# Loads, column halves and unit order of the first stage rewritten in a fused attention and feed-forward kernel

## The chip, the cores and the metric

The kernel runs on one Trainium2 chip, on all 8 cores at once; each core takes one batch element of 2048 tokens and runs the same program, with no exchange between cores. The metric is the device time in microseconds (us) of the slowest core. Lower is better.

## The reference

Per batch element, with 2048 tokens, width 1024, 16 heads of 64 and a hidden width of 3072:

```python
xn = _layernorm(x, axis=-1)
x = x + _L0_attn_ref(xn, W_attn, b_attn, W_proj, b_proj, temperature) + _L0_ffn_ref(xn, w_gate, w_up, w_down)
...
# attention: causal, with ALiBi slopes
qkv = x @ W_attn + b_attn
att = jnp.einsum('bqhd,bkhd->bhqk', q, k) * scale / temperature + bias
y = jnp.einsum('bhqk,bkhd->bqhd', softmax(att), v)
return y @ W_proj + b_proj
# feed-forward: weights are int8-valued integers times 1/127
h = _silu(x @ wg.T) * (x @ wu.T)
return h @ wd.T
```

## The kernel before, in words

The program has three stages. The **first stage** makes everything that attention starts from. The **second stage** (a long list of steps written by a planner, `attention_plan`) interleaves attention of 16 heads with 88 of the 96 gate-and-up units of the feed-forward part. The **third stage** is the output: the projection and the down product. The change touches the first stage and, on GpSimd, what the second one begins with.

In the first stage the 2048 tokens are 16 tiles of 128. For tile i the steps are these, each on another engine, tied by semaphores:

- SyncE loads the fp32 tile into one of four buffers `xstage` (semaphores `l_x0` to `l_x3`). Tile i, from 4 on, may be loaded once tile i-4 has been normalised (`v_xn`).
- VectorE takes the statistics (two `bn_stats`, one `bn_aggr`), ScalarE the square root into `sd`, VectorE the reciprocal into `rs`, and then it writes the normalised bf16 tile `xn_st`. Below this last one is called the normalisation of tile i.
- TensorE transposes the tile by eight matmuls with the identity into `ps_s` (even tiles) or `ps_gu` (odd ones): "transpose i", signalled by `p_xT`. ScalarE evacuates it into `xnT` (`a_xe`).
- TensorE multiplies 128 tokens of `xnT` by half of the value weights (512 columns of `wv_b`): a "V unit" of eight matmuls of 512 columns into `ps_t`. There are 32 of them, two halves for each of 16 tiles. ScalarE evacuates each into `Vt`.
- For every block of 512 tokens TensorE makes q and k of the first pair of heads from `wqk_b`: 16 matmuls, eight into `ps_m` and eight into `ps_y`, called QK 0 to QK 3. VectorE evacuates q (`evac_q`, `qst`), ScalarE k (`evac_k`, `kst`), and SyncE copies both to `qx` and `kx`.

All weights come by DMAs issued from GpSimd (POOL), which cast fp32 to bf16: the two halves of `wv_b` (128 x 4096 each), `wqk_b` for two pairs of heads, the first two sets of gate and up weights (`wgbuf`, `wubuf`), and `wpj_b` for the projection. GpSimd also sets constant rows of `qx` and `kx` by 12 memsets. The DMAs of SyncE and GpSimd are served by the same 16 DMA engines, from two queues.

Each engine runs its instructions in the order in which they are written, so the order of the code is the order of the work. Before the change, TensorE's loop does in pass i transpose i, then the V units of tile i-1; for tiles 0 to 3 only the first half, and their second halves together in pass 4, behind QK 0. ScalarE's loop does in pass i the square root of tile i, then the evacuation of transpose i-2. VectorE does in pass i the statistics of tile i, then the normalisation of tile i-1; `evac_q` stands behind the normalisations of tiles 5, 9 and 13 and at the end.

Of the kernel before, what the change touches and what calls it, by code (L numbers as in the profile page):

```python
# [11 lines left out]
I32 = mybir.dt.int32  # L12
AF = mybir.ActivationFunctionType
# [6 lines left out]
DC = C // 128  # L20
# [25 lines left out]
    "v_t", "v_cbq", "v_ln", "v_xn", "v_q", "v_mx", "v_mc", "v_m", "v_rc", "v_y", "v_h", "v_out",  # L46
# [108 lines left out]
def build_program(T):  # L155
# [28 lines left out]
    with st:  # L184
# [96 lines left out]
        v_at = {i: [(i - 1, 0)] for i in range(1, 5)}  # L281
        v_at[4] += [(tt, 1) for tt in range(4)]
        for i in range(5, NT + 1):
            v_at[i] = [(i - 1, 0), (i - 1, 1)]
        V0 = {i: sum(len(v_at[k]) for k in v_at if k < i) for i in range(NT + 3)}
# [37 lines left out]
        def _(e):  # L323
# [85 lines left out]
        def _(e):  # L409
# [8 lines left out]
            e.dma_start(out=bv_b[:, :], in_=battn_v[:, :]).then_inc(sem["l_bv"], 16)  # L418
            e.memset(Vt.rearrange("p (g d) -> p g d", d=VW)[:, :, 64:65], 1.0).then_inc(sem["g_set"], 1)
# [7 lines left out]
            for q in range(2):  # L427
                for j in range(2):
                    k = 1 + 3 * (2 * q + j)
                    e.wait_ge(sem["g_set"], k)  # L430
                    e.memset(qx[q][j][64:96, :], 1.0).then_inc(sem["g_set"], 1)
                    e.wait_ge(sem["g_set"], k + 1)
                    e.memset(kx[q][j][64:96, :], 0.0).then_inc(sem["g_set"], 1)
                    e.wait_ge(sem["g_set"], k + 2)
                    e.memset(kx[q][j][96:KT, :], 1.0).then_inc(sem["g_set"], 1)
# [16 lines left out]
            def gate_and_loads(f):  # L452
                silu(f)
                if f % 8 == 0 and f:
# [43 lines left out]
        def _(e):  # L498
# [21 lines left out]
            for i in range(NT + 1):  # L520
                if i < NT:
                    b = i % 4
                    e.wait_ge(sem[f"l_x{b}"], 16 * (i // 4 + 1))
                    for k in range(2):
                        e.bn_stats(st6[b][:, 6 * k:6 * k + 6], xstage[b][:, k * 512:(k + 1) * 512]).then_inc(  # L525
                            sem["v_ln"], 1)
                    e.wait_ge(sem["v_ln"], 4 * i + 1 if i else 2)
                    e.bn_aggr(mv[b][:, :], st6[b][:, :]).then_inc(sem["v_ln"], 1)
                if i:
                    b = (i - 1) % 4  # L530
                    e.wait_ge(sem["a_sd"], i)
                    e.reciprocal(rs[b][:, :], sd[b][:, :]).then_inc(sem["v_ln"], 1)
# [480 lines left out]
```

## Time and profile before

| | |
|---|---|
| three runs, median (lowest to highest) | 1139.33 us (1138.94 to 1139.5) |
| the profiled execution, its own time | 1137.8 us |
| span of its slowest core, core 2 | 1136.2 us |
| spans of its eight cores | 1131.2 to 1136.2 us |
| TensorE busy on core 2 | 1082.9 us, 95% of the span |
| VectorE, ScalarE, GpSimd busy | 55%, 42%, 29% |

A span goes from the first to the last instruction of a core; the time has 1.6 us around it. The busy share is an average over the three stages.

### The profile page before, as it was taken

How to read it: one execution, taken by the hardware profiler on the slowest of the kernel's cores; microseconds unless marked ns; L12 is line 12 of the kernel's file. 1: busy time of each engine (PE TensorE's matmuls, PEld its weight loads, DVE VectorE, ACT ScalarE, POOL GpSimd, SP SyncE). 2: the span in 40 equal slices, each digit the busy share in tenths (PEclk: the TensorE clock that was granted, in tenths of full speed). 3: DMA queues.
4: the chain of work that ended last, by engine and by line, in shares of the span. 5: the costliest groups of instructions: out<-in, count | busy, mean ns of one | idle time of the engine just before them, and what ended most of it. 6: DMA issues, size and time to landing. Idle time of an engine off the chain costs nothing.

```text
span 1136.2 us, 23969 instructions; the slowest of 8 cores (1131.2 to 1136.2 us)
## 1 busy us (share of the span) xinstructions
PE 1082.9 (95%) x7270; PEld 535.8 (47%) x7270; DVE 628.3 (55%) x1254; ACT 479.5 (42%) x869; POOL 332.8 (29%) x529
## 2 busy tenths in 40 slices
PE   2898899999999999999999999999999999999998
PEld 1444355545545555454554554455554344444443
DVE  4531867776776786787777678677882100001100
ACT  2443345655655565555565556556666200000000
POOL 7210112423332342233333233223333422222220
PEclk9999999999999999999999999999999999999999
DMA  8448032433412433143331213113521552525222
GB/s 191 141 93 169 16 62 67 79 72 71 84 41 65 84 81 67 39 85 67 71 57 33 64 38 67 32 33 69 173 61 54 203 190 74 185 74 185 74 77 72
DMA packets 57070, 98.34 MB, mean 87 GB/s; under 512 B 23292, under 2 KB 43909, under 8 KB 55862
## 3 DMA queue, kind: packets, MB, share of 16 engines
q0 software_dynamic: 7872, 35.66, 16.1%
q1 hardware_dynamic: 46178, 52.65, 15.7%
q10 hardware_dynamic: 2900, 8.51, 1.9%
q8 instruction: 66, 1.08, 0.4%
q14 instruction: 54, 0.44, 0.1%
HBM read 90.50 MB, written 27.26 MB: 104 GB/s over the span
## 4 chain that ended last, share of the span: by engine, by line
PE 87%; DVE 6%; issue 3%; DMA 2%; ACT 1%; POOL 1%; DVEq 0%; ACTq 0%; POOLq 0%; SPq 0%
PE ps_gu L752 25%; PE ps_dn L914 15%; PE ps_s L843 10%; PE ps_t L824 10%; PE ps_m L732 9%; PE ps_y L862 5%; PE ps_dn L909 5%; PE ps_t L792 5%; DVE cm L577 3%; PE ps_s L846 1%; DMA xstage<-xin 1%; DVE hst L513 1%; DMA tile_s<-tiles 1%; DVE qx L607 1%; DVE st L525 0%
## 5 line engine op out<-in xcount | busy, mean ns | idle before, releaser
L694 ACT ACTIVATE pt<-ps_t 128x512 bf16<-128x512 f32 (+1 forms) x576 | 328.6, 575 | 297.9 <-PE ps_t L824 283.2
L577 DVE TENSOR_REDUCE cm<-ps_s 128x1 f32<-128x512 f32 (+3 forms) x640 | 377.1, 607 | 136.4 <-PE ps_s L843 81.6
L752 PE MATMUL ps_gu<-xnT,wubuf 128*128 128x512 bf16 x768 | 261.5, 378 | 2.3 <-DVE hst L513 2.3
L752 PE MATMUL ps_gu<-xnT,wgbuf 128*128 128x512 bf16 x768 | 261.8, 378 | 1.2 <-ACT kst L638 1.2
L843 PE MATMUL ps_s<-kx,qx 67*128 67x512 bf16 (+3 forms) x640 | 215.6, 347 | 12.9 <-DVE cm L577 9.2
L824 PE MATMUL ps_t<-qx,kx 104*128 104x512 bf16 (+3 forms) x640 | 212.6, 348 | 5.2 <-DVE qx L607 4.4
L914 PE MATMUL ps_dn<-wdres,hb 128*128 128x512 bf16 x768 | 168.5, 379 | 0.0
L443 POOL TENSOR_SCALAR th_s<-th_s 128x512 f32<-128x512 f32 x96 | 59.4, 619 | 364.6 <-ACT th_s L646 364.0
L862 PEld LDWEIGHTS ps_y<-Vt,pt 128*128 128x128 bf16 x2176 | 121.5, 97 | 79.3 <-issue 0.9
L627 DVE SCALAR_TENSOR_TENSOR outsb<-ps_dn,xres 128x512 f32<-128x512 f32 x32 | 20.7, 687 | 205.1 <-PE ps_dn L914 205.1
L862 PE MATMUL ps_y<-Vt,pt 128*128 128x65 bf16 x2176 | 134.1, 193 | 0.0
L732 PE MATMUL ps_m<-xnT,wqk_b 128*128 128x512 bf16 x480 | 122.4, 379 | 0.0
L475 POOL TENSOR_SCALAR_AFFINE_SELECT pt<-pt 128x128 bf16<-128x128 bf16 x240 | 66.5, 294 | 180.1 <-ACT pt L694 179.3
L449 POOL TENSOR_TENSOR gs_s<-th_s,gh_s 128x512 bf16<-128x512 f32 x96 | 111.0, 1156 | 27.0 <-POOL th_s L443 22.9
L914 PEld LDWEIGHTS ps_dn<-wdres,hb 128*128 128x128 bf16 x768 | 75.1, 98 | 90.7
L843 PEld LDWEIGHTS ps_s<-kx,qx 67*128 67x128 bf16 x640 | 61.9, 97 | 113.6 <-issue 60.2
L752 PEld LDWEIGHTS ps_gu<-xnT,wubuf 128*128 128x128 bf16 x768 | 73.9, 98 | 58.1 <-issue 5.7
L752 PEld LDWEIGHTS ps_gu<-xnT,wgbuf 128*128 128x128 bf16 x768 | 74.5, 98 | 54.8 <-issue 2.0
L513 DVE SCALAR_TENSOR_TENSOR hst<-ps_gu,gs_s 128x512 bf16<-128x512 f32 x96 | 65.9, 686 | 40.1 <-POOL gs_s L449 31.3
L824 PEld LDWEIGHTS ps_t<-qx,kx 104*128 104x128 bf16 x640 | 61.0, 99 | 38.5 <-issue 13.0
L646 ACT ACTIVATE th_s<-ps_gu 128x512 f32<-128x512 f32 x96 | 57.0, 594 | 30.9 <-PE ps_gu L752 30.1
L792 PE MATMUL ps_t<-wv_b,xnT 128*128 128x512 bf16 x256 | 61.9, 398 | 4.0 <-DMA wv_b<-wv_r 2.5
(75 smaller groups left out, 707.9 us busy)
## 6 DMA issues: line engine op xcount, KB each, us to landing
h_sc<-hst SPq DMA_DIRECT2D x96, 128.0 KB, 1.9
hb<-h_sc SPq DMA_DIRECT2D x4, 3072.0 KB, 14.3
xstage<-xin SPq DMA_DIRECT2D x16, 512.0 KB, 6.2
xres<-xin POOLq DMA_DIRECT2D x16, 512.0 KB, 4.9
out<-outsb ACTq DMA_DIRECT2D x15, 512.0 KB, 3.0
wgbuf<-wg_r POOLq DMA_DIRECT2D x12, 512.0 KB, 5.3
wubuf<-wu_r POOLq DMA_DIRECT2D x12, 512.0 KB, 7.9
wd_sc<-wd_r POOLq DMA_DIRECT2D x12, 512.0 KB, 7.7
```

Of the source, the lines that this page charges most:

```text
L449: e.tensor_tensor(gs_s[f % 2][:, :], th_s[f % 2][:, :], gh_s[f % 2][:, :], AluOpType.mult).then_inc(sem["g_s"], 1)
L475: e.affine_select(pt[t % NPT][:, off:off + 128], pt[t % NPT][:, off:off + 128], [[1, 128]], AluOpType.is_ge, 0.0, base=0, channel_multipli ...
L513: e.scalar_tensor_tensor(hst[f % 4][:, :], ps_gu[:, 512:1024], 1.0 / 127.0, gs_s[f % 2][:, :], AluOpType.mult, AluOpType.mult).then_inc(se ...
L577: e.tensor_reduce(cm[:, c0:c0 + 1], ps_s[:, s % 2 * 512:s % 2 * 512 + w], AX.X, AluOpType.max, negate=True).then_inc(sem["v_mx"], 1)
L694: e.activation(pt[t % NPT][:, 0:w], ps_t[:, t % 2 * 512:t % 2 * 512 + w], AF.Exp).then_inc(sem["a_e"], 1)
L732: mm = e.matmul(ps[:, :], wqk_b[p % 2][:, f0 + dc * 256:f0 + dc * 256 + 128], xnT[:, dc * T + tc * 512:dc * T + (tc + 1) * 512], start=(dc ...
L752: mm = e.matmul(ps_gu[:, r // 8 * 512:r // 8 * 512 + 512], w[:, w0:w0 + 128], xnT[:, dc * T + tb * 512:dc * T + tb * 512 + 512], start=(dc ...
L792: mm = e.matmul(ps_t[:, n % 2 * 512:n % 2 * 512 + 512], xnT[:, dc * T + tt * 128:dc * T + (tt + 1) * 128], wv_b[:, half * 4096 + dc * 512: ...
L824: mm = e.matmul(ps_t[:, c0 + off:c0 + off + w], k_[0:KT, kt * 128:(kt + 1) * 128], q_[0:KT, b * 512 + i0 * 128:(b + 1) * 512], start=(x == ...
L843: mm = e.matmul(ps_s[:, r0:r0 + w], q_[0:KS, b * 512 + i * 128:b * 512 + (i + 1) * 128], k_[0:KS, c0:c0 + w], start=True, stop=not diag)
L862: mm = e.matmul(ps_y[:, i * VW:(i + 1) * VW], pt[a % NPT][:, c0:c0 + 128], Vt[:, (kt * H + h) * VW:(kt * H + h + 1) * VW], start=(T0[n] == ...
L914: return e.matmul(ps_dn[:, r0:r0 + 512], hb[tb % 2][:, hc * 512 + ts * 128:hc * 512 + ts * 128 + 128], wdres[:, hc * 1024 + half * 512:hc ...
```

## The change

SyncE loads tiles 0, 1 and 2 at once and tile 3 when the first quarter of the value weights has landed. GpSimd loads the value weights in four pieces of 2048 columns: the first when tile 0 has landed, the second when tile 1 has, then the q and k weights when the second piece has landed, then the last two pieces when those have. Of the 12 memsets, now written as 32-bit words (half as many elements), six follow there, and six after the loads of gate and up weights, set 0, and of q and k weights of the second pair. The loads of the second set of gate and up weights and of the projection weights move into the second stage, behind the first and the seventh gate-and-up unit. The V units of the first halves of tiles 0 to 7 come first, with the transposes up to tile 7 and QK 0 and QK 1 between them; the second halves of tiles 0 to 7 follow, with transposes 8 and 9, and from tile 8 on both halves of a tile, with its transpose two tiles ahead. ScalarE does one square root of a constant at its start.

```diff
+                if i == 3:
+                    e.wait_ge(sem["l_wva"], 16)
                 if i >= 4:
                     e.wait_ge(sem["v_xn"], i - 3)
                 e.dma_start(out=xstage[i % 4][:, :], in_=xin[i * 128:(i + 1) * 128, :]).then_inc(
                     sem[f"l_x{i % 4}"], 16)
-            e.wait_ge(sem["g_set"], 13)
+            e.wait_ge(sem["g_set"], 7)
...
             e.wait_ge(sem["l_x0"], 16)
+            e.dma_start(out=wv_b[:, 0:2048], in_=wv_r[0, :, 0:2048]).then_inc(sem["l_wva"], 16)
             e.wait_ge(sem["l_x1"], 16)
-            for half in range(2):
-                e.dma_start(out=wv_b[:, half * 4096:(half + 1) * 4096], in_=wv_r[half, :, :]).then_inc(
-                    sem[f"l_wv{half}"], 16)
-                if half == 0:
-                    cast_qk(0)
...
+            e.dma_start(out=wv_b[:, 2048:4096], in_=wv_r[0, :, 2048:4096]).then_inc(sem["l_wvb"], 16)
+            e.wait_ge(sem["l_wvb"], 16)
+            cast_qk(0)
+            e.wait_ge(sem["l_wq0"], 16)
+            e.dma_start(out=wv_b[:, 4096:6144], in_=wv_r[1, :, 0:2048]).then_inc(sem["l_wv1"], 16)
+            e.dma_start(out=wv_b[:, 6144:8192], in_=wv_r[1, :, 2048:4096]).then_inc(sem["l_wv1"], 16)
+            set_rows(0, 1)
             e.wait_ge(sem["v_xn"], NT - 4)
             cast_gu(0)
-            cast_gu(1)
             cast_qk(1)
-            e.dma_start(out=wpj_b[:, :], in_=wproj_r[:, :]).then_inc(sem["l_wp"], 16)
+            set_rows(1, 7)
...
+                if f == 0:
+                    cast_gu(1)
+                if f == 6:
+                    e.dma_start(out=wpj_b[:, :], in_=wproj_r[:, :]).then_inc(sem["l_wp"], 16)
...
+            statistics(2)
+            normalise(2)
+            statistics(3)
+            for i in range(3, NT):
+                if i + 1 < NT:
+                    statistics(i + 1)
+                normalise(i)
...
+                if i == 6:
+                    evac_q(0, 0)
+                if i == 8:
+                    evac_q(0, 1)
+                if i == 13:
+                    evac_q(0, 2)
...
+            for i in range(4, 8):
+                deviation(i)
+                evac_v(i - 2, i - 1)
+                if i == 6:
+                    evac_k(0, 0)
+                evac_x(i)
```

`deviation(i)` is the square root of tile i, `evac_x(i)` the evacuation of transpose i, `evac_v` those of V units.

TensorE, before the change, from its first transpose (`ps_s<-ident_s`, `ps_gu<-ident_s`: transposes of tiles 0, 1, 2 and so on; `ps_t<-wv_b`: V units, eight matmuls each; `ps_m` and `ps_y` from `wqk_b`: QK 0):

```order
L767 MATMUL ps_s<-ident_s,xn_st 128x128 x8
L767 MATMUL ps_gu<-ident_s,xn_st 128x128 x8
L792 MATMUL ps_t<-wv_b,xnT 128x512 x8
L767 MATMUL ps_s<-ident_s,xn_st 128x128 x8
L792 MATMUL ps_t<-wv_b,xnT 128x512 x8
L767 MATMUL ps_gu<-ident_s,xn_st 128x128 x8
L774 MATMUL ps_m<-c_s,onesf_s 128x1
L792 MATMUL ps_t<-wv_b,xnT 128x512 x8
L767 MATMUL ps_s<-ident_s,xn_st 128x128 x8
L792 MATMUL ps_t<-wv_b,xnT 128x512 x8
L732 MATMUL ps_m<-xnT,wqk_b 128x512 x8
L732 MATMUL ps_y<-xnT,wqk_b 128x512 x8
```

The same engine after the change, from transpose 4 to the second halves of the value weights:

```order
L829 MATMUL ps_s<-ident_s,xn_st 128x128 x8
L845 MATMUL ps_t<-wv_b,xnT 128x512 x8
L829 MATMUL ps_gu<-ident_s,xn_st 128x128 x8
L845 MATMUL ps_t<-wv_b,xnT 128x512 x8
L796 MATMUL ps_m<-xnT,wqk_b 128x512 x8
L796 MATMUL ps_y<-xnT,wqk_b 128x512 x8
L829 MATMUL ps_s<-ident_s,xn_st 128x128 x8
L845 MATMUL ps_t<-wv_b,xnT 128x512 x8
L829 MATMUL ps_gu<-ident_s,xn_st 128x128 x8
L845 MATMUL ps_t<-wv_b,xnT 128x512 x16
L796 MATMUL ps_m<-xnT,wqk_b 128x512 x8
L796 MATMUL ps_y<-xnT,wqk_b 128x512 x8
```

Eight V units and QK 0 and QK 1 now stand ahead of the first use of the second half of the weights, where four V units and QK 0 stood.

ScalarE before the change, from the square root of tile 4 (`sd`); `xnT<-ps_s` there is the evacuation of transpose 2:

```order
L663 ACTIVATE sd<-mv,eps_s 128x1
L666 ACTIVATE cvec_s<-ps_m 128x1
L670 ACTIVATE xnT<-ps_s 128x8x128
L678 ACTIVATE Vt<-ps_t 128x8x64
L663 ACTIVATE sd<-mv,eps_s 128x1
L670 ACTIVATE xnT<-ps_gu 128x8x128
L678 ACTIVATE Vt<-ps_t 128x8x64
```

ScalarE after it, from the evacuation of transpose 3 on:

```order
L696 ACTIVATE xnT<-ps_gu 128x8x128
L721 ACTIVATE cvec_s<-ps_m 128x1
L691 ACTIVATE sd<-mv,eps_s 128x1
L706 ACTIVATE Vt<-ps_t 128x8x64
L696 ACTIVATE xnT<-ps_s 128x8x128
L691 ACTIVATE sd<-mv,eps_s 128x1
L706 ACTIVATE Vt<-ps_t 128x8x64
L696 ACTIVATE xnT<-ps_gu 128x8x128
L691 ACTIVATE sd<-mv,eps_s 128x1
```

The square root of tile i+2 stood ahead of the evacuation of transpose i; now the evacuation of transpose i stands ahead of the square root of tile i+1.

GpSimd before the change, its loads and first memsets, with what each row waits for:

```order
L423 DMA wv_b<-wv_r 128x4096 [waits l_x0,l_x1]
L412 DMA wqk_b<-wqk_r 128x2048
L423 DMA wv_b<-wv_r 128x4096
L431 MEMSET qx 32x2048 [waits g_set]
L433 MEMSET kx 32x2048 [waits g_set]
L435 MEMSET kx 8x2048 [waits g_set]
```

GpSimd after it:

```order
L435 DMA wv_b<-wv_r 128x2048 [waits l_x0]
L437 DMA wv_b<-wv_r 128x2048 [waits l_x1]
L416 DMA wqk_b<-wqk_r 128x2048 [waits l_wvb]
L441 DMA wv_b<-wv_r 128x2048 [waits l_wq0]
L442 DMA wv_b<-wv_r 128x2048
L427 MEMSET qx 32x1024 [waits g_set]
L429 MEMSET kx 32x1024 [waits g_set]
L431 MEMSET kx 8x1024 [waits g_set]
```

The q and k weights and the last two pieces now wait for a landing, and the memsets stand behind them all.

## Rows read from the trace of the kernel before

**Rows 1.** Cores: span, mean granted TensorE clock, of two cores
```profile
core 2: 1136.2 us, clock 0.997
core 3: 1131.2 us, clock 0.998
```

**Rows 2.** Timeline: first gate matmul on core 2, then core 3 (start us, us, engine, line)
```profile
112.89 0.38 PE L752 MATMUL ps_gu<-xnT,wgbuf 128*128 128x512 bf16 x1 [1.25 <-ACT kst L638]
...
108.02 0.38 PE L752 MATMUL ps_gu<-xnT,wgbuf 128*128 128x512 bf16 x1 [1.25 <-ACT kst L638]
```

**Rows 3.** TensorE's waits, core 2, 0 to 113 us: total, times, longest
```profile
PE ps_s L767 <- DVE xn_st L536: 15.3, 2, 11.5
PE ps_gu L767 <- DVE xn_st L536: 5.1, 1, 5.1
PE ps_s L767 <- ACT xnT L670: 4.0, 2, 2.0
```

**Rows 4.** Chain that ended last, first stage: start us, us, what
```profile
17.55 12.71 DMA xstage<-xin
...
41.64 6.91 PE ps_t L792 x32
...
64.15 0.45 PE ps_gu L767 x8
...
74.13 5.30 PE ps_t L792 x16
```

**Rows 5.** Timeline: issue of the first and the second half of the value weights
```profile
9.23 0.54 POOL L423 DMA_DIRECT2D wv_b<-wv_r  x1 [5.72 <-DMA xstage<-xin]
...
10.28 0.55 POOL L423 DMA_DIRECT2D wv_b<-wv_r  x1
```

**Rows 6.** Issue to landing: first value half, q and k, second half; then tile 13
```profile
DMA to landing us min/median/max: 11.8/11.8/11.8
...
DMA to landing us min/median/max: 15.7/15.7/15.7
...
DMA to landing us min/median/max: 23.7/23.7/23.7
...
DMA to landing us min/median/max: 3.3/3.3/3.3
```

**Rows 7.** DMA queues, 20 to 30 us: packets, MB, share of 16 engines
```profile
q0 software_dynamic: 230, 1.28, 77.5%
q1 hardware_dynamic: 227, 0.80, 26.4%
```

**Rows 8.** Timeline, 53 to 54 us: one square root, evacuation, reciprocal, normalisation
```profile
53.04 0.28 ACT L663 ACTIVATE sd<-mv,eps_s 128x1 f32<-128x1 f32 x1
53.22 1.01 ACT L670 ACTIVATE xnT<-ps_s 128x1024 bf16<-128x1024 f32 x1
53.42 0.16 DVE L532 RECIPROCAL rs<-sd 128x1 f32<-128x1 f32 x1 [0.93 <-ACT sd L663]
53.76 0.81 DVE L536 TENSOR_SCALAR xn_st<-xstage,mv,rs 128x1024 bf16<-128x1024 f32 x1 [0.18 <-DVE rs L532]
```

**Rows 9.** Timeline: memsets on GpSimd and the normalisation beside them
```profile
13.21 1.80 POOL L433 MEMSET kx<- 32x2048 bf16 x1
14.96 2.52 DVE L536 TENSOR_SCALAR xn_st<-xstage,mv,rs 128x1024 bf16<-128x1024 f32 x1
```

**Rows 10.** Timeline of the first V unit; five microseconds with the granted clock (PEclk)
```profile
21.16 3.17 PE L792 MATMUL ps_t<-wv_b,xnT 128*128 128x512 bf16 x8 [2.52 <-DMA wv_b<-wv_r]
...
75.00:80.00 5.00, 5.00 (x23) 2.21 (x22) 4.55 (x9) 2.22 (x5) 3.28 (x6) 0.66 0.78 203
```

**Rows 11.** Statistics of tiles 0 and 1 waiting for their loads; landing of projection weights
```profile
6.38 1.29 DVE L525 BATCH_NORM_STATS2 st<-xstage 128x6 f32<-128x512 f32 x2 [4.93 <-DMA xstage<-xin]
...
8.78 1.29 DVE L525 BATCH_NORM_STATS2 st<-xstage 128x6 f32<-128x512 f32 x2 [0.80 <-DMA xstage<-xin]
...
DMA to landing us min/median/max: 31.3/31.3/31.3
```

More of the change, by code:

```diff
@@ L278, in gu_of @@
             return (f // 4, f % 4) if f < NF_ATT else (f // 8 * 2 + f % 2, f % 8 // 2)
[L281 to L285, printed above, removed]
+        v_units = [(tt, 0) for tt in range(8)] + [(tt, 1) for tt in range(8)]
+        v_units += [(tt, half) for tt in range(8, NT) for half in range(2)]
         FM = [NF_ATT * 16 * (k + 1) // len(steps) for k in range(len(steps))]
@@ L427, in _ @@
[L427 to L435, printed above, removed]
+            e.dma_start(out=wv_b[:, 2048:4096], in_=wv_r[0, :, 2048:4096]).then_inc(sem["l_wvb"], 16)
@@ new lines, in _ @@
+            statistics(0)
+            statistics(1)
+            normalise(0)
+            normalise(1)
+            e.wait_ge(sem["l_const"], 16 * 5)
+            e.tensor_scalar(t8_s[0:1, :], temp_s[0:1, :], 8.0, None, AluOpType.mult).then_inc(sem["v_t"], 1)
+            e.wait_ge(sem["v_t"], 2)
+            e.reciprocal(c11_s[0:1, :], t8_s[0:1, :]).then_inc(sem["v_t"], 1)
+            statistics(2)
[5 more added lines that the diff above has]
+                normalise(i)
@@ L680, in _ @@
                                  AF.Copy).then_inc(sem["a_v"], 1)
-                    if i == 6 and x == 0:
-                        evac_k(0, 0)
-                if i >= 11 and i % 4 == 3:
-                    evac_k(0, i // 4 - 1)
+            deviation(0)
+            deviation(1)
+            evac_x(0)
+            evac_x(1)
+            deviation(2)
+            evac_v(0, 1)
+            deviation(3)
+            evac_v(1, 2)
+            evac_x(2)
+            evac_x(3)
+            e.wait_ge(sem["p_c"], 1)
+            e.activation(cvec_s[:, :], ps_m[:, 0:1], AF.Copy).then_inc(sem["a_c"], 1)
+            for i in range(4, 8):
[4 more added lines that the diff above has]
+                evac_x(i)
+            evac_v(6, 7)
+            deviation(8)
+            evac_v(7, 8)
+            evac_k(0, 1)
+            evac_v(8, 9)
+            deviation(9)
+            evac_v(9, 11)
+            evac_x(8)
+            evac_v(11, 13)
+            deviation(10)
+            evac_v(13, 14)
+            evac_x(9)
+            evac_v(14, 16)
+            for i in range(8, NT):
+                if i + 3 < NT:
+                    deviation(i + 3)
+                if i + 2 < NT:
+                    evac_x(i + 2)
+                evac_v(2 * i, 2 * i + 2)
+                if i == 12:
+                    evac_k(0, 2)
             evac_k(0, NTB - 1)
@@ L796, in _, with first_qk @@
                     mm.then_inc(sem["p_v"], 1)
-                if i >= 9 and i % 4 == 1:
-                    tc = i // 4 - 1
+            def first_qk(tc):
+                e.wait_ge(sem["a_xe"], 4 * tc + 4)
+                if tc == 0:
+                    e.wait_ge(sem["l_wq0"], 16)
+                    e.wait_ge(sem["a_c"], 1)
+                else:
                     e.wait_ge(sem["v_q"], tc)
                     e.wait_ge(sem["a_k"], tc)
-                    q_or_k(0, 2 * tc, ps_m, range(DC)).then_inc(sem["p_qk"], 1)
-                    q_or_k(0, 2 * tc + 1, ps_y, range(DC)).then_inc(sem["p_qk"], 1)
+                q_or_k(0, 2 * tc, ps_m, range(DC)).then_inc(sem["p_qk"], 1)
+                q_or_k(0, 2 * tc + 1, ps_y, range(DC)).then_inc(sem["p_qk"], 1)
+            e.wait_ge(sem["l_id"], 16)
+            transpose_x(0)
+            transpose_x(1)
+            values(0, 2)
+            transpose_x(2)
+            transpose_x(3)
+            e.wait_ge(sem["v_t"], 3)
+            e.wait_ge(sem["l_const"], 16 * 5)
+            e.matmul(ps_m[:, 0:1], onesf_s[0:1, :], c11_s[0:1, :], start=True, stop=True).then_inc(
+                sem["p_c"], 1)
+            for i in range(4, 8):
+                values(i - 2, i - 1)
+                if i == 6:
+                    first_qk(0)
+                transpose_x(i)
+            values(6, 8)
+            first_qk(1)
+            e.wait_ge(sem["l_wv1"], 32)
+            values(8, 11)
+            transpose_x(8)
+            values(11, 14)
+            transpose_x(9)
+            values(14, 16)
+            for i in range(8, NT):
+                if i + 2 < NT:
+                    transpose_x(i + 2)
+                values(2 * i, 2 * i + 2)
+                if i == 11 or i == 15:
+                    first_qk(i // 4)
             e.wait_ge(sem["v_q"], NTB)
```

133 lines of the change are left out of this document (61 added, 72 removed), and 2 rows, old and new, of the table SEMS.

## The prediction

> **What bounds the kernel now.** I read the spans of the cores first, then the timeline at the border of the first two stages. Core 2 ends at 1136.2 us and core 3 at 1131.2 [rows 1]; their first gate matmuls, the start of the second stage, stand at 112.89 and 108.02 [rows 2]. The differences are 1023.3 and 1023.2 us, and the other six cores give the same within 0.1. So everything behind the first stage takes 1023.3 us whatever happened before, and a microsecond won or lost in the first stage is one in the time. The slowest core sets it, so I work on core 2.
>
> What the first stage must cost TensorE comes from the chain of waits [rows 4]: a transpose is 0.45 us, four V units 6.91, so 1.73 each, and a QK, twice eight matmuls of the same shape, 3.46. 16 transposes, 32 V units and 4 QK are 7.2 + 55.4 + 13.8 = 76.4 us. The stage ends at 112.9, so 36.5 us are something else. Most is at the front. At 41.64 us, when QK 0 is done [rows 4], TensorE has done 5 transposes, 4 V units and QK 0, 12.6 us of work: it is 29.0 us behind. TensorE's waits [rows 3] say for what: 15.3 and 5.1 us for normalised tiles, and the chain shows the load of tile 5 behind them, 12.71 us from 17.55 [rows 4], while a tile loaded alone lands in 3.3 [rows 6]. Value weights arriving at the same time slow it: in 20 to 30 us both queues are served, packet for packet [rows 7]. Behind 41.64 another 112.9 - 76.4 - 29.0 = 7.5 us go: two waits of 2.0 behind QK 1 and QK 2 for a transposed tile to be evacuated [rows 3], 1.25 for the last evacuation of k [rows 2], and 1.85 where two V units took 5.30 instead of 3.45 [rows 4], the granted clock being 0.66 in the mean there [rows 10], part of it at the lower of its two levels, 1.2 GHz instead of 2.4.
>
> **The change, part by part.** *Weights.* The first half was issued at 9.23 and landed 11.8 later, at 21.0; the q and k weights, half as large and issued half a microsecond behind, at 25.5 (15.7 from issue); the second half at 10.28 + 23.7 = 34.0 [rows 5, 6]. So a piece of half a megabyte takes 4.3 us of a shared queue, and the first has 11.8 - 8.5 = 3.3 on top. Now the first piece is issued when tile 0 lands, 6.4 [rows 11], and lands at 6.4 + 3.3 + 4.3 = 14.0; the second at 18.3. The q and k weights wait for that and land 7.6 later, 25.9; the last pieces at 33.5 and 37.8. Waiting for landings costs 3.3 us twice; the cover is that nothing reads those last pieces before QK 1 has ended, 10 us later (below).
>
> *Tiles.* Tile 3 is issued at 14.0 and not at 2.5, and tile 4 behind it on SyncE's queue. Tiles 0 and 1 landed 2.4 us apart [rows 11]. Beside weights a tile took up to 12.7, alone 3.3. Packets of the two queues alternate, 230 to 227 [rows 7], and the new pieces have rows half as long, so a tile gets through in about one piece, 4.3 us. I take 5 us for tile 3, 19.0, and 21.4 for tile 4. The statistics of tile 4 stand ahead of the normalisation of tile 3: 1.3 + 0.2 + 0.2 + 0.8 and hand-offs of 0.3 put transpose 3 at 24.2. V units 0 and 1 run before it, 12 matmuls after 18.3 at the slow pace of the first V unit, eight in 3.17 [rows 10]: 4.8 us, hidden.
>
> The Trainium skill, page "DMA: Bandwidth & Descriptors", section "Queues, rings and completion order", says that a DMA engine takes turns between the queues at packet granularity. By that rule, the trace agrees. Were shares by bytes, tiles would go on taking 10 to 12 us beside weights, and the sum would be that of the rival "late tiles" below.
>
> *A new chain.* On ScalarE the square root of tile i+1 now stands behind the evacuation of transpose i. So transpose i+1 follows transpose i by 0.45 (transpose) + 1.01 (evacuation) + 0.28 (root) + 0.16 (reciprocal) + 0.81 (normalisation) = 2.7 [rows 4, 8], and five hand-offs of some 0.14 (0.18 behind the reciprocal, rows 8): 3.4 us. TensorE has 0.45 + 1.73 = 2.2 between two of them, so it idles 1.2 us between 3 and 4, 4 and 5, 6 and 7; QK 0 covers 5 to 6. Transpose 4: tile 5 lands about 25.7, its statistics let tile 4 be normalised at 27.9, so 28.1. Transpose 5: 31.5. Transpose 6: 31.5 + 0.45 + 1.73 + 3.46 = 37.1. Transpose 7: 40.5; tile 8, whose statistics stand ahead of it, is issued at 28 beside weights and lands about 28 + 3.3 + 4.3 = 35.6, in time. Then 0.45, two V units and QK 1: 47.9.
>
> *Memsets.* Twelve of them followed the issue of the loads, one after another, and a normalisation that met one took 2.52 us instead of 0.81 [rows 8, 9]. Now six stand behind 26 us. Half the elements: between 0.9 us each (half of 1.80) and 1.80. They may lengthen up to three normalisations, 0 to 3 us; I take 0.5, for most of the time VectorE waits for tiles. Six more come later, under continuous V units.
>
> *From there.* Done at 48.4: 8 transposes, 8 V units, QK 0 and 1, 24.4 us, so TensorE is 24.0 behind. 52.0 us of work are left. Transposes run two tiles ahead, and 8 and 9 have three V units, 5.2 us, in front of them, above the chain's 3.4, so no idling. QK 1 is followed by V units whose inputs are there: its wait of 2.0 goes. Behind QK 2, VectorE still evacuates q before it normalises tile 14, and transpose 14 follows QK 2: 2.0 stays. 1.25 at the end stays. I keep one stretch at the lower clock, 1.85 [rows 4], against such a stretch here and one more near 35 us. 48.4 + 52.0 + 2.0 + 1.25 + 1.85 = 105.5.
>
> *Second stage.* The second gate and up set and the projection weights now load there. Behind it: three issues of GpSimd, 0.54 each [rows 5], on an engine 29% busy; the set is first read at unit 8, the projection weights in the third stage. About 3 MB at 8.5 us each are 26 us of a queue. I cost it at nothing; bare, the landing of 31.3 us [rows 11] is the most that one reader could wait. The gate set 0, issued when tile 11 is normalised, has 30 us and more to land. The early square root takes nothing from the path, since landings bound the start.
>
> **Sum.** 112.9 - 105.5 = 7.4 us: 5.0 from the front (29.0 to 24.0), 2.0 from the wait behind QK 1, 0.4 from the rest. The profiled execution, 1137.8, becomes 1130.4. The median of the runs is 1.5 above it: 1131.9.
>
> **The rivals.** *Late tiles, faster by less.* If tiles beside weights still take 10 us or more, transposes 3 to 7 come 4 to 5 us later: 1136. For it: 12.71 us [rows 4]. Against it: smaller packets, and between 14 and 26 us only one piece at a time is in the queue. *More gain.* If the chain's hand-offs hide (3 x 1.2 = 3.6) and no stretch is slow (1.85): 5.5 more, 1126.4. Against it: ScalarE's order is fixed. *Slower: the clock.* TensorE works in bursts with waits up to 40 us. If the clock stays at 1.2 GHz from transpose 3 to QK 1, 5 transposes, 6 V units and two QK, 19.6 us, take 39.2: QK 1 ends at 63.4, the stage at 118.7, the time is 1145. It decides once the slow work costs more than the 7.4 won. Against it: the first V unit was slow, but work at full pace followed soon, with gaps as large. The Trainium skill, "TensorE: Matmul & The Clock Gate", section "HAM oscillation", tells of short bursts between waits for data that fall to the lower clock each time; by that rule this rival would hold, and the trace shows it only after single waits [rows 10]. *Slower: moved loads.* 26 us of queue in the second stage, if a third of it met a store or a copy that an engine waits for, would eat the gain; nothing in the trace waits so. *No change* would need losses that happen to match: the 1023.3 us speak against cover elsewhere.
>
> **How the numbers follow.** Within 0.2%, 2.3 us, this kernel's measurement tells nothing. Forecast, 1129 to 1135: 0.60. More gain: 0.14. Late tiles: 0.11. Within 0.2%: 0.06. Slower, clock 0.05 and loads 0.04: 0.09. So faster 0.85, same 0.06, slower 0.09. The range takes in most of the more-gain case and late tiles: 1126.5 to 1137.
>
> **What would show it.** The first gate matmul at 105 to 106 us on the slowest core and the same 1023.3 behind it; first piece landed at 14, transpose 3 at 24, waits of 1.2 us for a normalised tile ahead of transposes 4, 5 and 7, QK 1 ending at 48, no wait behind it and one of 2 us behind QK 2. It is wrong if that remainder grows, if V units up to 48 us run at 3.4 us each, or if tiles land over 8 us after issue between 14 and 30 us.

## The result and the profile after

The median went from 1139.13 to 1134.43 us, a ratio of 0.996 with a 95% interval of 0.9945 to 0.9975: 4.7 us faster (2.8 to 6.3), where 1131.9 was forecast. The profiled execution took 1134.53 us and its span is 1133.0, on core 3. In every execution the time is the slowest core's span and 1.5 to 1.6 us. In some executions the cores of one die show a lower granted clock and the time is longer; ratios and means here leave them out, the medians count them, which moves only that of e4 by more than 0.2 us (1141.57 without them). The mean of the eight spans scatters less than the slowest: it is 1130.4 us after, and 1134.2 over the 47 executions of the kernel before that were measured beside the experiments, so 3.8 us less. I give it as "mean core" for each experiment.

The page of the kernel after, its span and busy times:

```profile
span 1133.0 us, 23997 instructions; the slowest of 8 cores (1128.6 to 1133.0 us)
...
PE 1083.7 (96%) x7270; PEld 535.3 (47%) x7270; DVE 629.2 (56%) x1254; ACT 481.4 (42%) x870; POOL 322.1 (28%) x531
```

Two of its cores (span, mean granted clock of TensorE), and the first gate matmul in the timelines of core 3 and core 2:

```profile
core 2: 1128.6 us, clock 0.998
core 3: 1133.0 us, clock 0.998
```

```profile
107.80 0.38 PE L816 MATMUL ps_gu<-xnT,wgbuf 128*128 128x512 bf16 x1 [1.25 <-ACT kst L666]
...
103.45 0.38 PE L816 MATMUL ps_gu<-xnT,wgbuf 128*128 128x512 bf16 x1 [1.25 <-ACT kst L666]
```

Against [rows 1, 2] the first stage of the slowest core ends 5.1 us earlier, 107.8 for 112.9, and 110.3 became 105.2 in the mean over the cores. But 1133.0 - 107.80 = 1025.2 and 1128.6 - 103.45 = 1025.15: the remainder, 1023.3 before, has grown by 1.9 on every core. 5.1 - 1.9 = 3.2 is what the two profiled spans differ by.

Now the front of the first stage, from the timeline of core 3 (start, duration, engine, line; in brackets the idle time before and what ended it). Rows between these are left out:

```profile
15.39 1.86 PE L845 MATMUL ps_t<-wv_b,xnT 128*128 128x512 bf16 x4 [1.98 <-DMA wv_b<-wv_r]
...
18.23 4.42 PE L845 MATMUL ps_t<-wv_b,xnT 128*128 128x512 bf16 x12 [0.98 <-DMA wv_b<-wv_r]
...
18.63 0.53 POOL L416 DMA_DIRECT2D wqk_b<-wqk_r  x1 [9.34 <-DMA wv_b<-wv_r]
...
19.56 1.29 DVE L537 BATCH_NORM_STATS2 st<-xstage 128x6 f32<-128x512 f32 x2 [3.59 <-DMA xstage<-xin]
...
22.89 1.29 DVE L537 BATCH_NORM_STATS2 st<-xstage 128x6 f32<-128x512 f32 x2 [1.73 <-DMA xstage<-xin]
...
25.79 0.61 PE L829 MATMUL ps_gu<-ident_s,xn_st 128*128 128x128 bf16 x8 [2.68 <-DVE xn_st L550]
...
29.34 0.61 PE L829 MATMUL ps_s<-ident_s,xn_st 128*128 128x128 bf16 x8 [0.81 <-DVE xn_st L550]
...
30.84 0.53 POOL L441 DMA_DIRECT2D wv_b<-wv_r  x1 [11.68 <-DMA wqk_b<-wqk_r]
...
31.93 0.94 POOL L427 MEMSET qx<- 32x1024 int32 x1
31.97 1.46 DVE L550 TENSOR_SCALAR xn_st<-xstage,mv,rs 128x1024 bf16<-128x1024 f32 x1 [0.24 <-DVE rs L545]
...
33.68 0.61 PE L829 MATMUL ps_gu<-ident_s,xn_st 128*128 128x128 bf16 x8 [2.00 <-DVE xn_st L550]
...
36.41 1.64 DVE L550 TENSOR_SCALAR xn_st<-xstage,mv,rs 128x1024 bf16<-128x1024 f32 x1 [0.24 <-DVE rs L545]
...
42.92 0.61 PE L829 MATMUL ps_gu<-ident_s,xn_st 128*128 128x128 bf16 x8 [1.29 <-DVE xn_st L550]
...
50.27 5.34 PE L845 MATMUL ps_t<-wv_b,xnT 128*128 128x512 bf16 x24
...
86.64 1.01 PE L829 MATMUL ps_s<-ident_s,xn_st 128*128 128x128 bf16 x8 [2.44 <-DVE xn_st L550]
87.45 4.84 PE L845 MATMUL ps_t<-wv_b,xnT 128*128 128x512 bf16 x16
```

Each wait of TensorE can be read off, and each has its cause beside it. The last but two is the end of QK 1: V units follow at 50.27 with no idle time in front, so the wait of 2.0 behind QK 1 [rows 3] is gone. Behind QK 2 one of 2.44 stayed, and the two V units after it took 4.84 instead of 3.46, at the lower clock for a while (granted clock 0.63 from 86 to 88 us, 0.52 from 88 to 90), as [rows 4] show for before. All eight cores have the wait of 2.44; cores 1, 3, 6 and 7 have the slow stretch, which lengthens the way from transpose 14 to QK 3 from 14.7 to 16.3 or 16.4 us.

TensorE's waits from 0 to 112 us (engine, buffer, line, releaser: total, times, longest), to be set against [rows 3]:

```profile
PE ps_s L829 <- DVE xn_st L550: 14.6, 3, 11.3
PE ps_gu L829 <- DVE xn_st L550: 6.0, 3, 2.7
PE ps_t L845 <- DMA wv_b<-wv_r: 3.0, 2, 2.0
PE ps_gu L816 <- ACT kst L666: 1.2, 1, 1.2
```

11.3 is the start, before the first tile can be transposed. The rest is now short waits, each under 3 us.

### The profile page after: what moved, and what is told of

The parts are those of the page before. It is cut to its first block, busy times and chain, and to the rows that moved or that the text cites. A ratio compares the mean times of both kernels' runs of the same rounds, so it can differ in the third digit from the quotient of the medians.

```text
span 1133.0 us, 23997 instructions; the slowest of 8 cores (1128.6 to 1133.0 us)
## 1 busy us (share of the span) xinstructions
PE 1083.7 (96%) x7270; PEld 535.3 (47%) x7270; DVE 629.2 (56%) x1254; ACT 481.4 (42%) x870; POOL 322.1 (28%) x531
## 3 DMA queue, kind: packets, MB, share of 16 engines
q0 software_dynamic: 8160, 35.66, 16.3%
q1 hardware_dynamic: 46178, 52.65, 15.4%
## 4 chain that ended last, share of the span: by engine, by line
PE 87%; DVE 5%; issue 3%; DMA 2%; ACT 1%; POOL 1%; DVEq 0%; SPq 0%; POOLq 0%; ACTq 0%
PE ps_gu L816 25%; PE ps_dn L1003 15%; PE ps_s L932 11%; PE ps_t L913 10%; PE ps_m L796 9%; PE ps_y L951 5%; PE ps_dn L998 5%; PE ps_t L845 4%; DVE cm L605 3%; DMA xstage<-xin 2%; PE ps_s L935 1%; DVE hst L526 1%; DMA wv_b<-wv_r 1%; DVE qx L635 1%; PE ps_y L796 0%
```

## The experiments

Twelve kernels. The median, the ratio to the kernel before with its interval, the mean core, and the range over the cores of the remainder (span less first gate matmul, from the profiled execution):

| kernel | median us | ratio | mean core | remainder |
|---|---|---|---|---|
| before | 1137.7 to 1139.4 | 1 | 1134.2 | 1023.2 to 1023.3 |
| after | 1134.43 | 0.996 (0.9945 to 0.9975) | 1130.4 | 1025.1 to 1025.2 |
| e1 | 1134.57 | 0.9975 (0.9965 to 0.9985) | 1130.6 | 1024.9 to 1025.1 |
| e2 | 1139.43 | 1.0009 (1.0 to 1.0019) | 1134.1 | 1023.3 to 1023.8 |
| e3 | 1132.55 | 0.995 (0.9934 to 0.9965) | 1128.0 | 1025.0 to 1025.2 |
| e4 | 1142.11 | 1.0028 (1.0016 to 1.0041) | 1138.4 | 1024.9 to 1025.4 |
| e5 | 1129.64 | 0.9929 (0.9913 to 0.9946) | 1126.4 | 1024.9 to 1025.3 |
| e6 | 1142.29 | 1.003 (1.0018 to 1.0042) | 1137.7 | 1023.0 to 1023.6 |
| e7 | 1137.95 | 0.9991 (0.9981 to 1.0001) | 1133.8 | 1024.8 to 1025.1 |
| p1 | 1138.51, one | none | 1133.6 | 1023.2 to 1023.5 |
| p2 | 1139.22 | 1.0012 (1.0002 to 1.0021) | 1135.6 | 1024.9 to 1025.3 |
| p3 | 1139.21, one | none | 1135.4 | 1024.2 to 1024.9 |
| c1 | 1128.24 | 0.9911 (0.9896 to 0.9926) | 1124.3 | 1024.9 to 1025.0 |
| c2 | 1127.46 | 0.9902 (0.9886 to 0.9917) | 1124.0 | 1023.8 to 1024.2 |

On two cores each of after, e1, e3, e4, e5, e7, c1 and c2 the trace lacks the record of the first gate matmul, and the remainder would read half a microsecond short; they are left out of the ranges.

### Where the 1.9 us of the second stage come from

**e1: the moved loads put back.** The second gate and up set and the projection weights go back to the first stage; all else as after.

```diff
             cast_gu(0)
+            cast_gu(1)
             cast_qk(1)
+            e.dma_start(out=wpj_b[:, :], in_=wproj_r[:, :]).then_inc(sem["l_wp"], 16)
...
                 silu(f)
-                if f == 0:
-                    cast_gu(1)
-                if f == 6:
-                    e.dma_start(out=wpj_b[:, :], in_=wproj_r[:, :]).then_inc(sem["l_wp"], 16)
```

> The changed kernel with the second gate and up set and the projection weights loaded in the first stage again, right behind set 0. In the changed kernel, span minus first gate matmul is 1025.2 us on every core, 1.9 more than before. Theory A (the moved loads did that: GpSimd's issues in the second stage shift it against VectorE): the remainder is 1023.3 again, the first stage is unchanged (first gate matmul at 103.5 to 107.8 us over the cores), the time is about 1132.5. Rival B (the memsets, the first stage's end or mere phase did it): the remainder stays at 1025.2 and the time at 1134.4.

The remainder stayed near 1025 and the time at that of after, as the rival said. **e2** is the other half: the kernel before with only these loads moved, as above with the signs turned.

> The kernel before with nothing but those two loads moved: gate and up set 1 behind unit 0, the projection weights behind unit 6. Theory A: the remainder behind the first gate matmul grows from 1023.3 to 1025.2, the first stage ends where it did (108 to 113 us over the cores), the time is 1.9 above before, about 1141. Rival B: the remainder stays at 1023.3 and the time at 1139.1.

Its remainder is 1023.3 to 1023.5 (one core 1023.8) and its mean core is that of before. So the loads cost at most 0.2 us, and my first theory, that the loads moved behind the border cost the 1.9, fell. The edit costed at nothing does cost nothing; what grew the remainder is elsewhere.

I then set the second stages of before and after against each other, matmul by matmul, both counted from the first gate matmul. Up to 304 us behind it they keep step within some 0.1 us except at three places, the same on all cores: at 114, 139 and 304 us the kernel after falls back by 0.35, 0.9 and 0.7. Later they drift by up to 0.5 both ways and end 1.9 apart. The order of instructions is the same there. The first place, in the timeline of core 2 before:

```profile
225.07 0.54 POOL L475 TENSOR_SCALAR_AFFINE_SELECT pt<-pt 128x128 bf16<-128x128 bf16 x2 [0.78 <-ACT pt L694]
225.20 0.19 DVE L597 CAST nm<-nmf 128x4 bf16<-128x4 f32 x1 [0.17 <-DVE nmf L588]
```

and of core 3 after:

```profile
220.09 0.54 POOL L488 TENSOR_SCALAR_AFFINE_SELECT pt<-pt 128x128 bf16<-128x128 bf16 x2 [0.79 <-ACT pt L758]
220.59 0.17 DVE L625 CAST nm<-nmf 128x4 bf16<-128x4 f32 x1 [0.54 <-DVE nmf L616]
```

In both, VectorE's small cast comes right after GpSimd's two selects have begun. In before it starts 0.13 us behind them and runs beside them; in after it starts 0.50 behind, when they are nearly through, 0.54 instead of 0.17 after its input. That looks like a race with GpSimd, but its input is ready 0.04 us ahead of the selects in both (225.03 and 225.07, 220.05 and 220.09): nothing changed between the two engines, and only VectorE's cast is held up 0.37 longer. The second place, core 2 before and then core 3 after:

```profile
250.50 0.17 DVE L599 TENSOR_TENSOR nm<-cm,nm 128x4 bf16<-128x4 f32 x1
250.70 0.70 DVE L607 TENSOR_TENSOR qx<-ps_m,tile_s 8x512 bf16<-8x512 f32 x1
250.73 1.16 POOL L449 TENSOR_TENSOR gs_s<-th_s,gh_s 128x512 bf16<-128x512 f32 x1 [0.57 <-ACT pt L694]
```

```profile
245.67 1.15 POOL L458 TENSOR_TENSOR gs_s<-th_s,gh_s 128x512 bf16<-128x512 f32 x1 [0.27 <-POOL th_s L452]
245.75 1.09 DVE L627 TENSOR_TENSOR nm<-cm,nm 128x4 bf16<-128x4 f32 x1
...
246.88 0.70 DVE L635 TENSOR_TENSOR qx<-ps_m,tile_s 8x512 bf16<-8x512 f32 x1
```

Counted from the first gate matmul, GpSimd's product starts at 137.8 or 137.9 in both, while `nm` comes 0.34 later in after, by the first step. In before GpSimd's product had stood idle 0.57 and came behind `nm`; in after it stood 0.27 and got 0.08 ahead, and the tiny `nm` then took 1.09 instead of 0.17 and ended with it. `qx`, for which TensorE waits, followed. So the second place reads as a race of VectorE and GpSimd, decided by 0.3 us of idle time of GpSimd that is gone. What moves such idle times? After has 4 more instructions on TensorE, 16 on VectorE, 1 on ScalarE, 5 on GpSimd and 2 on SyncE, most of them waits that are long fulfilled.

**p1, p2, p3: waits that wait for nothing.** The kernel before, with repeated waits on semaphores that have long been reached. p2 has as many on each engine as after has more; p1 has TensorE's alone, p3 VectorE's alone.

```diff
-            e.wait_ge(sem["l_id"], 16)
+            for _ in range(5):
+                e.wait_ge(sem["l_id"], 16)
...
+            for _ in range(16):
+                e.wait_ge(sem["v_t"], 3)
             evac_q(0, NTB - 1)
```

> The kernel before with four more waits on TensorE's queue at the very start, on a semaphore that has been reached (5 instead of 1). The changed kernel has four instructions more on TensorE ahead of the second stage than before, 16 on VectorE, 1 on ScalarE, 5 on GpSimd, 2 on SyncE. Theory C (the 1.9 us in the second stage come from where its instructions stand in TensorE's stream: one matmul 21.4 us behind the first gate matmul starts 0.1 later with no visible releaser, and VectorE then loses races against GpSimd for the right to run): remainder behind the first gate matmul 1025 instead of 1023.3, with steps of 0.4, 0.9 and 0.7 at 114, 139 and 304 us. Rival D (the order of the work itself, not its place in the stream): the remainder stays at 1023.3.

> The kernel before with as many idle waits on each engine as the changed kernel has more instructions there ahead of the second stage: 4 on TensorE, 16 on VectorE, 1 on ScalarE, 5 on GpSimd, 2 on SyncE; nothing else differs. Theory C in its wider form (place in the streams of all engines): remainder about 1025 with the steps at 114, 139 and 304 us, time 1.7 above before, 1139.7 to 1140.8. Rival D: remainder 1023.3, time as before.

> The kernel before with only the 16 idle waits on VectorE. All five engines padded gave a remainder of 1025.0 behind the first gate matmul, TensorE's four alone 1023.4. Theory (the place in VectorE's stream is what counts): 1025.0 with steps at 114, 139 and 304 us. Rival (it is GpSimd's, ScalarE's or SyncE's stream): 1023.4.

p2 has no other work and no other order than before, and its remainder is 1025.0, with the steps at the places of after; its mean core rose by 1.5 us, and its median from the 1137.68 of the kernel before beside it to 1139.22. At the first place its timeline (core 2) reads as that of after, the cast 0.50 behind the selects:

```profile
223.29 0.54 POOL L477 TENSOR_SCALAR_AFFINE_SELECT pt<-pt 128x128 bf16<-128x128 bf16 x2 [0.79 <-ACT pt L699]
223.79 0.17 DVE L601 CAST nm<-nmf 128x4 bf16<-128x4 f32 x1 [0.54 <-DVE nmf L592]
```

TensorE's four alone did nothing (1023.4). VectorE's sixteen alone gave 1024.2 (one core 1024.9), with the first and third steps but not the second, where I had expected all three. That the count or the place of instructions in the streams, without any change of the work, makes 1.7 of the 1.9 us is shown.

The traces say more. In p3 all four engines start their work within 0.01 us of before, counted from the first gate matmul, for almost 40 us: the waits left no delay behind them that could travel on. Then VectorE's `qst` starts 0.35 earlier than in before. Core 2 before, and core 1 of p3 (their first gate matmuls at 112.89 and 113.39):

```profile
152.65 0.81 DVE L503 TENSOR_SCALAR qst<-ps_m,cvec_s,cbq_s 128x512 bf16<-128x512 f32 x1 [1.34 <-PE ps_m L732]
```

```profile
152.80 0.81 DVE L503 TENSOR_SCALAR qst<-ps_m,cvec_s,cbq_s 128x512 bf16<-128x512 f32 x1 [0.99 <-PE ps_m L734]
```

A hold-up of 0.35 us ahead of `qst` is gone, and one of the same size stands ahead of the cast of the first place. The DMA queues show what goes with it: a transfer of 8 KB on a queue that the profile calls "instruction", so by its name one that loads the program's code. In before (core 2) one starts from 153 to 154 us, and in p3 (core 1) one from 226 to 227:

```profile
q14 instruction: 1, 0.01, 3.3%
```

```profile
q14 instruction: 1, 0.01, 2.5%
```

On all eight cores of before and of p3 such a transfer starts 0.55 to 0.9 us behind the instruction that was held up, and there is none at the place where the other kernel has it. The same holds for GpSimd's product at the second place: in before it stood 0.57 with such a transfer behind it, in after and p2 0.27 with none. At the third place VectorE's cast stood 0.52 in p3 and after and 0.17 in before, but no such transfer starts within a microsecond of it; 0.35 late, it and the product behind it ran beside GpSimd's work and took 0.31 and 0.48 instead of 0.17 each.

The stream of the second step can be read as well, and is GpSimd's: in e6 below GpSimd has four more instructions and VectorE none, and 0.3 us of idle time have moved from GpSimd's product to the operation before it; in c2 GpSimd has five more and VectorE none, and of the three steps only the second is left. So in the streams of these two engines there are points at which the next instruction comes 0.3 to 0.35 us late, and more instructions ahead shift other work onto them. That the loading of code is the cause is argued from the transfers that go with most of them; no run changed it by itself, and none padded GpSimd alone.

### What the gain of the first stage rests on

**e6: only the new loads.** The kernel before with the new weights' pieces, their waits for landings and the held tile 3, but with the old order on the engines and the old memsets.

```diff
+                if i == 3:
+                    e.wait_ge(sem["l_wva"], 16)
...
+            e.dma_start(out=wv_b[:, 0:2048], in_=wv_r[0, :, 0:2048]).then_inc(sem["l_wva"], 16)
             e.wait_ge(sem["l_x1"], 16)
+            e.dma_start(out=wv_b[:, 2048:4096], in_=wv_r[0, :, 2048:4096]).then_inc(sem["l_wvb"], 16)
+            e.wait_ge(sem["l_wvb"], 16)
             cast_qk(0)
+            e.wait_ge(sem["l_wq0"], 16)
```

> The kernel before with the changed loads alone (tile 3 held, four pieces, GpSimd's waits for landings, the last pieces behind the q and k weights), the old order of units, roots and evacuations, the old memsets. Theory (the loads' gain at tiles 4 to 7 is lost, since the old order wants the second half of the value weights right behind QK 0): transposes 3 and 4 come some 3 us earlier, TensorE waits for the last pieces behind QK 0 instead, the stage ends within 2 us of before, 1137 to 1140. Rival (the loads do it all): the gain of the whole change, 1133 to 1135.

It is slower than before, 3.0 us in the mean core against the kernel before measured beside it, and a little slower than the 1137 to 1140 that I expected. Core 6 shows where, in its waits and its timeline: the old order wants the second half of the value weights behind QK 0, and the new loads bring it late.

```profile
PE ps_t L797 <- DMA wv_b<-wv_r: 8.5, 2, 5.1
```

```profile
42.30 4.42 PE L797 MATMUL ps_t<-wv_b,xnT 128*128 128x512 bf16 x10 [5.10 <-DMA wv_b<-wv_r]
```

**e4: the new order, weights not held.** The two waits for landings ahead of the q and k weights and of the last pieces are taken out of after.

```diff
-            e.wait_ge(sem["l_wvb"], 16)
             cast_qk(0)
-            e.wait_ge(sem["l_wq0"], 16)
```

> The changed kernel without the two waits of GpSimd for landings (second piece, q and k weights): the five weight loads are issued back to back from 9 to 11 us, and the six memsets follow at once. Theory (holding the weights back is what lets tiles 4 to 7 land early): tiles issued between 14 and 30 us take 8 us or more again, transposes 4 to 7 come later, QK 1 ends 3 to 6 us later and the time is 2 to 6 us higher, 1137 to 1140. Rival (the waits only cost their fixed 3.3 us each and the order of units does the rest): q and k weights land at 26 and the last pieces at 34 to 35 instead of 31 and 42, nothing waits for them anyway, and the time stays within 1 us.

Slower than before too, and some 7 us above after (mean core +8.0), more than the 2 to 6 expected. The DMA queues from 20 to 30 us, first after (core 3), then e4 (core 5), as [rows 7] for before:

```profile
q1 hardware_dynamic: 498, 1.79, 59.4%
q0 software_dynamic: 144, 0.52, 32.2%
```

```profile
q0 software_dynamic: 291, 1.05, 65.6%
q1 hardware_dynamic: 330, 1.22, 34.1%
```

Holding the weights halves what their queue moves there, and the tiles' queue moves half as much again. In e4's timeline (core 5) tile 3, which after's statistics had at 19.56, comes at 25.12, and transpose 3 at 32.60 behind a wait of 8.8:

```profile
25.12 1.29 DVE L535 BATCH_NORM_STATS2 st<-xstage 128x6 f32<-128x512 f32 x2 [8.59 <-DMA xstage<-xin]
...
32.60 1.01 PE L827 MATMUL ps_gu<-ident_s,xn_st 128*128 128x128 bf16 x8 [8.77 <-DVE xn_st L548]
```

**e7: tile 3 not held.** After without SyncE's wait ahead of tile 3.

```diff
-                if i == 3:
-                    e.wait_ge(sem["l_wva"], 16)
```

> The changed kernel without holding tile 3 back for the first piece. Theory (tile 3 is not needed before V units 0 and 1 are done, but ahead of the pieces it delays them): the first piece lands 1 to 2 us later, the second too, tiles 4 and 5 are issued 2.5 us earlier and land earlier by less; the time within 1 us of the changed kernel. Rival (holding it matters as the landing waits do): 2 us or more slower.

3.5 us slower than after (mean core +3.4), where I had expected less than 1: the rival held. The timeline of core 5 shows both pieces of the value weights late, 16.80 and 21.89 where core 3 of after had 15.39 and 18.23:

```profile
16.80 1.87 PE L843 MATMUL ps_t<-wv_b,xnT 128*128 128x512 bf16 x4 [3.78 <-DMA wv_b<-wv_r]
...
21.89 4.92 PE L843 MATMUL ps_t<-wv_b,xnT 128*128 128x512 bf16 x12 [3.22 <-DMA wv_b<-wv_r]
```

Where the pieces land differs from core to core (on core 2 of after the first V unit began at 12.92 and the second piece came at 18.32), so the two rows show the direction, and the mean core the size. So new loads without the order, and the order without the held loads, both lose; the gain needs both.

**e3: the root ahead of the evacuation.** On ScalarE the square root of tile i+1 stands in front of the evacuation of transpose i, for tiles 4 to 8.

```diff
             evac_x(2)
+            deviation(4)
             evac_x(3)
...
-                deviation(i)
                 evac_v(i - 2, i - 1)
...
+                deviation(i + 1)
                 evac_x(i)
```

> The changed kernel with ScalarE's square root of tile i+1 ahead of the evacuation of transpose i (tiles 4 to 8). Theory (the new chain transpose, evacuation, root, normalisation paces transposes 3 to 7 at 3.4 us or more): TensorE's waits of 1.3 us ahead of transposes 5 and 7 shrink to nothing, QK 1 ends some 2.5 us earlier and the time is 1 to 2.5 us lower. Rival (the landings of tiles pace them): the waits move from ScalarE to the loads and the time stays within 0.7 us.

1132.55, 1.9 us below after, and 2.4 in the mean core. The chain that I had read was real and could be cut: QK 1 ends at 45.7 us in the mean over the cores, where after has 48.6, and on core 1 transposes wait less,

```profile
PE ps_gu L829 <- DVE xn_st L550: 3.0, 3, 2.0
```

3.0 us where core 3 of after has 6.0. What is left there, 1.96, comes behind a normalisation that met a memset and took 1.67 us.

**e5: q evacuated one tile later.** VectorE normalises tile 14 before it evacuates q of QK 2.

```diff
-                if i == 13:
+                if i == 14:
                     evac_q(0, 2)
```

> The changed kernel with VectorE's evacuation of the third q behind the normalisation of tile 14 instead of ahead of it. Theory (the wait of 2.0 to 2.4 us behind QK 2, and the stretch at the lower clock that can follow it, come from that order): no wait of TensorE behind QK 2, the first gate matmul 2 us earlier on every core and up to 3.8 on cores that had the slow stretch there, time 1131 to 1132.5. Rival (the landing of tiles 14 and 15 would hold it up next): gain below 0.7 us.

1129.64 us, 4.8 below after, 4.0 in the mean core, and below the 1131 to 1132.5 expected. From the end of QK 1 to the first gate matmul, after has 55.8 us on the cores without the slow stretch and 57.3 to 57.5 on those with it; e5 has 53.2 on all. So the wait is worth 2.6 us on each core and the slow stretch 1.7 on four of eight, 3.4 together in the mean and 4.3 on a slow core. The rest is the front, which e5 does not touch: QK 1 ended 0.7 earlier in its profiled execution. The slowest core of e5, without wait or slow stretch:

```profile
82.49 0.61 PE L829 MATMUL ps_s<-ident_s,xn_st 128*128 128x128 bf16 x8
82.94 3.62 PE L845 MATMUL ps_t<-wv_b,xnT 128*128 128x512 bf16 x16
```

All eight cores have a granted clock of 1.000 over the whole span, where six of after's eight were at 0.997 or 0.998: four by the stretch behind QK 2, and two by one at the front, which e5's edit does not reach.

**c1 and c2: a version that beats both.** c1 is e3 and e5 together. c2 is c1 without one wait of VectorE in each normalisation, for the aggregate that the square root has already waited for:

```diff
                 e.wait_ge(sem["v_rs"], i + 1)
-                e.wait_ge(sem["v_ag"], i + 1)
```

> Both the root ahead of the evacuation and the late evacuation of the third q. If the two terms are of different places they add: the root alone gave about 1.9 us, the q about 2.0 to 2.5, so 1130 to 1131 against 1134.4 of the changed kernel. Rival: they share a limit (the supply of tiles) and the sum is no better than the better one alone.

> Root first and late q, and VectorE's wait on v_ag ahead of each normalisation left out (the square root it has already waited for was taken behind that same signal), which gives VectorE as many instructions ahead of the second stage as before the change. If the remainder hangs on VectorE's count: 1023.3 instead of 1025.0, so 1126.5 against 1128.2. If it hangs on another engine's stream: 1025.0 and 1128.2.

c1's mean core is 6.1 below after's, the sum of e3's 2.4 and e5's 4.0 within 0.3, and its median is better than the 1130 to 1131 expected. c2 got the remainder down to 1023.8 to 1024.2, between its theory and its rival: the first and third steps are gone (at the first place the cast again starts 0.14 behind the selects) and the second stayed, so taking 16 instructions from VectorE's stream undoes just what putting 16 in did in p3. Its 1127.46 is the best time of the study, 1.0% below the kernel before. From c1 it can't be told apart by time: the mean cores are 0.3 apart, since c2's first stage ended a microsecond later in its profiled execution.

## Why the prediction was right, and where it was off

**Sign and range.** Faster, inside the range, 2.5 us above the forecast. The forecast's sum was made on the profiled execution, 1130.4 against 1134.5 measured, 4.1 short; the median of before was 1.5 above its profiled time and that of after 0.1 below, which gives 1.6 back. That is luck of which execution was profiled, so the sum missed by more than the forecast did: 7.4 us were to be won in the profiled span, and 3.2 were.

**First stage, 105.5 against 107.8.** The mechanisms were as forecast (measured, and forecast in brackets): first piece at 15.4 (14.0), second at 18.2 (18.3), tile 3 at 19.6 (19.0), transpose 3 at 25.8 (24.2), waits for normalised tiles ahead of transposes 4, 5 and 7 of 0.81, 2.00 and 1.29 (1.2 each), nothing behind QK 1, 2.44 behind QK 2 (2.0), 1.25 at the end. The memsets took 0.94, the lower of my two bounds, and 1.32 beside a normalisation. The size was off at one step, the front: QK 1 ended at 50.3 instead of 48.4. Tile 4 landed at 22.9 instead of 21.4 and carried transposes 3 and 4 with it; then two normalisations met memsets and took 1.46 and 1.64 instead of 0.81, 1.5 us for which I had put 0.5. My reason for so little, that VectorE mostly waits for tiles there, didn't hold: from transpose 4 on it was VectorE's chain that TensorE waited for. Behind 50.3 the sum holds: 52.0 + 2.4 + 1.25 + 1.4 gives 107.4, against 107.8.

**"Costs 1.2 three times", the chain.** e3 cut it and gained some 2 us of the 3.6, so the reading was right for the larger part. **"2.0 stays behind QK 2", and one slow stretch.** e5 removed both. The wait was worth 2.6 for 2.0, and the stretch, 1.7 for 1.85, belonged to it on the four cores that had it. The prediction counted them as two terms, where one cause gave both, and the second not on every core.

**"A queue serves packet for packet".** It held in before (230 to 227, [rows 7]) and so for tiles 3 and 4, but the q and k weights needed 12.2 us from issue to landing (18.63 to 30.84) instead of 7.6, with 498 packets of the tiles' queue to 144 of the weights'. That cost nothing, since nothing read them before 35.8, as nothing read the last pieces before QK 1 had ended. The waits for landings, which I had priced at 3.3 us twice and hidden, were hidden, and e4 shows that the change doesn't pay without them.

**"Second stage: I cost it at nothing."** The loads did cost nothing (e1, e2), but the remainder grew by 1.9, the sign that I had named for being wrong. The step that failed was the first one, "a microsecond won or lost in the first stage is one in the time": true of one program whose cores start the second stage at different times, and not across two programs. p2 shows it without any change of work: 1025.0.

**The rivals.** Late tiles: those of e4, 1142, are what not holding the weights would have given; in after tile 3 came 4.2 us after its issue at 15.33. The clock: on core 3 it fell only after the wait behind QK 2, at a cost of 1.4 us. The twelve matmuls from 18.23 were slow too (4.42 us, though the granted clock reads 1.00 there), but those between 26 and 50 us ran at full pace (1.89 for eight) between waits of 0.8 to 2.0. Core 4 shows the rival for six microseconds, just where it was placed. It waited 3.56 us for transpose 3, and the next V unit took 3.60 us, at a granted clock of 0.50 from 22 to 26 us (its row of stages, the clock the third number from the end):

```profile
22.50 1.01 PE L829 MATMUL ps_gu<-ident_s,xn_st 128*128 128x128 bf16 x8 [3.56 <-DVE xn_st L550]
...
23.96 3.60 PE L845 MATMUL ps_t<-wv_b,xnT 128*128 128x512 bf16 x8
```

```profile
22.00:26.00 4.00, 3.50 (x15) 2.00 (x16) 2.43 (x6) 1.27 (x3) 0.15 (x1) 0.50 0.86 196
```

Core 2 had the same behind a wait of 3.55 for the second piece (0.57 from 18 to 22 us). So the rival did come true for a stretch on two of eight cores. On core 3 it did not, though that core waited 2.68 us for transpose 3. "HAM oscillation" in the Trainium skill's page "TensorE: Matmul & The Clock Gate" was the basis for it. The example there has longer waits than these 0.8 to 2.0 us between its bursts, so by that section the rival did not follow for them; the traces agree with it on cores 2 and 4, where a long wait did come.

## What to carry to other kernels

Loads that run beside each other share a queue's time, so order them by when they are read, hold back those that are read late, and change the order of the reading engines with them: here the held loads alone lost 3 us, and the order with loads not held some 4, each against the kernel before. When one engine waits 2 us in the middle of dense work, look who was served first on the engine that it waits for; moving that one evacuation behind the normalisation gave 2.6 us on every core, and 1.7 more where the wait had been followed by the lower clock. And before a microsecond in a stage that was not touched is explained by what was moved, pad the kernel before with idle waits to the new instruction counts: here that alone made 1.7 of the 1.9 us.

## What the runs showed of the hardware

Waits that are already fulfilled, in the first stage, made the second 1.7 us longer (1023.3 to 1025.0, p2), at fixed places more than 100 us later, the same on all eight cores. An engine's next instruction can come 0.3 to 0.35 us late at points that shift with the number of instructions ahead of it; at three of the four looked at (`qst` and the first cast on VectorE, `gs_s` on GpSimd) a transfer of the queue "instruction" starts 0.55 to 0.9 us later, at the fourth (the cast 302 us behind the gate matmul) none does. VectorE and GpSimd can hold each other up: a 128x4 product begun 0.08 behind GpSimd's product of 1.15 took 1.09 instead of 0.17, and a normalisation took 1.46 and 1.64 instead of 0.81 beside memsets of 0.94. That the two engines share a way into memory would fit both, and was not tested by itself. The weights' queue, with one transfer in flight at a time, moved 0.52 MB in 10 us beside the tiles, and with several 1.05 (e4) and 1.28 MB (before, [rows 7]): its share of the engines went with how much stood in it.
